# The first FFN's residual sum in a fused transformer-like kernel: one VectorE operation becomes a ScalarE and a GpSimd one

## The reference

```python
x = x + 0.5 * ffn(layernorm(x))
x = x + attn(layernorm(x))          # gated convolution, linear recurrence, product, residual, layernorm * ln_w + ln_b
x = x + 0.5 * ffn(layernorm(x))     # the same weights
# ffn: router logits -> sigmoid + bias -> best 2 of 4 groups -> best 4 of 32 experts, weights scaled by 2.5
#      sum over all chosen experts of w * down(silu(gate x) * (up x)), inner size 64, plus one shared expert of inner size 128
```

## Time and profile before

| | us |
|---|---|
| median of 3 runs | 675.33 (675.2 to 675.62) |
| the profiled execution | 675.38 |
| its span, first to last instruction | 673.6 |
| TensorE busy in it | 659.0 (98%) |
| VectorE busy | 550.5 (82%) |
| ScalarE busy | 421.5 (63%) |
| GpSimd busy | 446.5 (66%) |

### The profile page before, as it was taken

The page is one execution under the profiler, slowest core; times in us unless marked ns, Lnnn a source line. Parts: engine busy times, 40 slices in busy tenths (PEclk is TensorE's granted clock), DMA queues, the critical chain, the costliest instruction groups (busy, mean ns, idle before and its releaser), DMA issues. The chain is left out here.

```text
span 673.6 us, 10309 instructions
## 1 busy us (share of the span) xinstructions
PE 659.0 (98%) x3071; PEld 532.7 (79%) x3071; DVE 550.5 (82%) x1540; ACT 421.5 (63%) x804; POOL 446.5 (66%) x452
## 2 busy tenths in 40 slices
PE   7999999999999999999999999999999999999997
PEld 6877888888888887888878888888878778777685
DVE  5788889988978887889779898688979868867765
ACT  3766576675576656666567765757576566655553
POOL 2256558775676776866767766878676776776563
PEclk7999999999999999999999999999999999999999
DMA  7752908429092834719074370916519064380561
GB/s 191 168 139 68 224 4 195 91 71 199 5 210 72 185 85 96 159 58 224 20 176 111 89 166 26 228 35 154 116 30 221 5 157 108 76 184 17 119 135 32
DMA packets 60232, 78.30 MB, mean 116 GB/s; under 512 B 8176, under 2 KB 27664, under 8 KB 60176
## 3 DMA queue, kind: packets, MB, share of 16 engines
q1 hardware_dynamic: 60176, 77.65, 51.6%
HBM read 74.49 MB, written 3.15 MB: 115 GB/s over the span
## 5 line engine op out<-in xcount | busy, mean ns | idle before, releaser
L578 POOL TENSOR_TENSOR hid_lo<-hid,hid_hi 128x512 fp32r<-128x512 f32 x270 | 348.3, 1294 | 191.5 <-ACT hid_hi L690 191.3
L837 DVE TENSOR_TENSOR weighted<-gate_ps,raw 128x512 f32<-128x512 f32 x256 | 175.3, 685 | 69.3 <-ACT gate_ps L682 62.0
L682 ACT ACTIVATE gate_ps<-gate_ps 128x512 f32<-128x512 f32 x256 | 148.7, 581 | 120.0 <-PE gate_ps L1116 116.6
L690 ACT ACTIVATE hid_hi<-hid 128x512 fp32r<-128x512 f32 x272 | 170.5, 627 | 62.6 <-DVE hid L850 59.3
L850 DVE TENSOR_TENSOR hid<-weighted,up_ps 128x512 f32<-128x512 f32 x256 | 174.3, 681 | 7.5
L1177 PE MATMUL down_ps<-hid_lo,wt_hi 128*128 128x512 f32 x272 | 107.8, 396 | 0.2 <-DVE hid_lo L858 0.2
L1174 PE MATMUL down_ps<-hid_hi,wt_hi 128*128 128x512 f32 x272 | 107.7, 396 | 0.0
L1175 PE MATMUL down_ps<-hid_hi,wt_lo 128*128 128x512 f32 x272 | 107.5, 395 | 0.0
L1114 PE MATMUL gate_ps<-xT_hi,wt_hi 128*128 128x512 f32 x170 | 71.7, 422 | 0.0
L1114 PE MATMUL up_ps<-xT_hi,wt_hi 128*128 128x512 f32 x170 | 68.2, 401 | 2.1 <-DVE hid L850 2.1
L1115 PE MATMUL gate_ps<-xT_lo,wt_hi 128*128 128x512 f32 x170 | 67.2, 395 | 0.0
(11 more groups left out here) (183 smaller groups left out, 1114.6 us busy)
## 6 DMA issues: line engine op xcount, KB each, us to landing
raw<-wT_hbm SPq DMA_DIRECT2D x96, 512.0 KB, 11.4
raw<-wT_hbm SPq DMA_DIRECT2D x62, 256.0 KB, 4.6
x_ln<-in_L_attn_x SPq DMA_DIRECT2D x8, 256.0 KB, 4.0
x_res<-in_L_attn_x SPq DMA_DIRECT2D x8, 256.0 KB, 3.7
out_x<-x SPq DMA_DIRECT2D x7, 256.0 KB, 2.3
raw<-in_L_ffn_gate_w SPq DMA_DIRECT2D x4, 256.0 KB, 5.2
raw<-in_L_ffn_up_w SPq DMA_DIRECT2D x4, 256.0 KB, 4.4
raw<-in_L_ffn_down_w SPq DMA_DIRECT2D x4, 256.0 KB, 4.7
```

What stands on the lines that cost most here:

```text
L578: nc.gpsimd.tensor_tensor(hid_lo[s][:, :], hid[s][:, :], hid_hi[s][:, :].bitcast(F32), ALU.subtract)\
L682: nc.scalar.activation(bank[:, :] if j else silu_sb[:, :], bank[:, :], ACT.Silu).then_inc(silu_done, 1)
L690: nc.scalar.activation(hid_hi[s][:, :], hid[s][:, :], ACT.Copy).then_inc(hid_hi_done, 1)
L837: V.tensor_tensor(weighted[j % 2][:, :], gate_ps[n % BANKS][:, :], wb[:, j - 1, :], ALU.mult)\
```

## The change

ScalarE reads `side` with a factor 0.5 into a new SBUF tile `first_half`; GpSimd adds `x_res` to it. VectorE's operation goes. TensorE's next use of `side` waits for ScalarE's read in place of VectorE's sum. In the tables, "add ffn 1" goes to the next whole slot, and in units (1,1) and (1,2) the steps from "stats 2" to "normalise 2" (in (1,2) to "transpose 2") go to later slots.

```diff
-        ADD = {"copy ffn 1": 1, "transpose ffn 1": 4, "add ffn 1": 8.5}
+        ADD = {"copy ffn 1": 1, "transpose ffn 1": 4, "add ffn 1": 9, "halve ffn 1": 5}
...
# BEGIN, unit (1,1), block 0
-                ({"copy ffn 1": 2, "transpose ffn 1": 3, "add ffn 1": 5.5}, 0),
-                ({"stats 2": 5.5, "meanvar 2": 5.5, "norm 2": 6, "normalise 2": 7, "transpose 2": 10, "xT high 2": 10,
+                ({"copy ffn 1": 2, "transpose ffn 1": 3, "add ffn 1": 6, "halve ffn 1": 4}, 0),
+                ({"stats 2": 7.5, "meanvar 2": 7.5, "norm 2": 8, "normalise 2": 9, "transpose 2": 10, "xT high 2": 10,
...
# BEGIN, unit (1,2), block 1
-                ({"copy ffn 1": 3, "transpose ffn 1": 4, "add ffn 1": 4.5}, 1),
-                ({"stats 2": 5.5, "meanvar 2": 5.5, "norm 2": 6, "normalise 2": 7, "transpose 2": 8, "xT high 2": 10,
+                ({"copy ffn 1": 3, "transpose ffn 1": 4, "add ffn 1": 5, "halve ffn 1": 5}, 1),
+                ({"stats 2": 6.5, "meanvar 2": 6.5, "norm 2": 7, "normalise 2": 8, "transpose 2": 9, "xT high 2": 10,
...
# BEGIN, unit (1,3), block 2
-                ({"copy ffn 1": 1, "transpose ffn 1": 4, "add ffn 1": 3.5}, 2),
+                ({"copy ffn 1": 1, "transpose ffn 1": 4, "add ffn 1": 5, "halve ffn 1": 5}, 2),
...
# END, unit (4,4), block 7
-                ({"copy ffn 1": 3, "transpose ffn 1": 4, "add ffn 1": 6.5}, 7),
+                ({"copy ffn 1": 3, "transpose ffn 1": 4, "add ffn 1": 7, "halve ffn 1": 5}, 7),
...
# GpSimd, behind "norm 2" and ahead of "add ln_b"
+                    for b in due(steps, "add ffn 1", j):
+                        pool.wait_ge(x_res_loaded, b * 16 + 16)
+                        pool.wait_ge(first_halved, b + 1)
+                        if b >= 2:
+                            pool.wait_ge(x1_b_done, b - 1)
+                            pool.wait_ge(ln_normed[2], b - 1)
+                        nc.gpsimd.tensor_tensor(x1[b % 2][:, :, :], first_half[:, :, :], x_res[:, :, :], ALU.add)\
+                          .then_inc(ffn_added[1], 1)
...
# ScalarE, behind "xT high 1" and ahead of "copy ffn 1"
+            def halve_first(b):
+                act.wait_ge(ffn_transposed[1], b + 1)
+                if b > 0:
+                    act.wait_ge(ffn_added[1], b)
+                nc.scalar.activation(first_half[:, :, :], side_td, ACT.Copy, scale=0.5).then_inc(first_halved, 1)
...
# VectorE
-                for b in due(steps, "add ffn 1", slot):
-                    dve.wait_ge(x_res_loaded, b * 16 + 16)
-                    dve.wait_ge(ffn_transposed[1], b + 1)
-                    if b >= 2:
-                        dve.wait_ge(x1_b_done, b - 1)
-                    V.scalar_tensor_tensor(x1[b % 2][:, :, :], side_td, 0.5, x_res[:, :, :], ALU.mult, ALU.add)\
-                     .then_inc(ffn_added[1], 1)
...
# TensorE
-                        side_read = (ffn_added[1], b + 1)
+                        side_read = (first_halved, b + 1)
```

More of the change, by code:

```diff
@@ L208, in macaron_kernel @@
         ffn_half = sb("ffn_half", [P, TT, P])
+        first_half = sb("first_half", [P, TT, P])
         gate_t = sb("gate_t", [P, BLK])
@@ L297, in macaron_kernel @@
         halved_done = sem("halved_done")
+        first_halved = sem("first_halved")
         y_hi_done = sem("y_hi_done")
@@ L751, in unit @@
                         xT_high(1, b)
+                    for b in due(steps, "halve ffn 1", j):
+                        halve_first(b)
                     for b in due(steps, "copy ffn 1", j):
```

## The result

The changed kernel took 678.84 us (median of 5 runs, 677.4 to 679.54) against 675.33 us before: ratio 1.0052, 95% interval 1.0041 to 1.0063, so 3.5 us slower. It lies in the range given, one microsecond above the number predicted; two of the five executions, the profiled one among them, lie above the range's end of 679.2.

The account below looks back on a forecast made before the run. TensorE, almost never idle, was taken to bound the kernel, so only its waits count. The terms 2.4 + 0.4 - 0.3 gave +2.5 us on the profiled 675.38, so 677.9, with a range of 675.0 to 679.2.

Parts of the forecast that it names:

- What bounds the kernel: Whole kernel: TensorE is busy 659.0 of 673.6 us, so time freed on VectorE is worth nothing by itself.
- The shared-table units, 0: The four units of blocks 3 to 6: idle time covers the added operations; 0, bounds 0 to 0.2 us each.
- The second rival: Shared-table units: GpSimd's additions hold VectorE's operation with two SBUF inputs, 4 x 0.6 us, total 680.3; chance 0.04.
- the rule of the Trainium skill: VectorE operations with both inputs in SBUF and GpSimd instructions reading SBUF share a read interface; the later one is blocked.
- Unit (1,2), the main term: Unit (1,2): TensorE waits for "normalise 2" before "transpose 2"; +2.4 us, bounds 1.6 to 3.3.
- GpSimd is in time: Unit (1,2): GpSimd has "norm 2" done at 129.75, before "normalise 2" starts on ScalarE at 129.87.
- Behind the wait everything on the other engines catches up, so I count it once: Unit (1,2): the 2.4 us wait is counted once, as the other engines catch up behind it.
- the upper bound of 3.3: Unit (1,2): the term's upper limit, should late silu and weighting cause a second wait at tile 11.
- Unit (1,1): Unit (1,1): "transpose 2", due at 89.81, waits for "normalise 2" until 90.2; +0.4 us, bounds 0 and 1.0.
- Unit (4,4): Unit (4,4): the bank is read earlier, so "mixer out" no longer waits; -0.3 us, bounds -0.5 and +0.3.
- No wait at all (1): Units (1,2) and (1,1): no wait, time stays or falls by the 0.3 of (4,4), 675.1; chance 0.13.
- VectorE the real pace (3): Whole kernel: VectorE sets the pace, TensorE's records hide it, and 5.5 us come back, 669.9; chance 0.04.

Follow-up runs that it names:

- The doubling: The changed kernel with ScalarE's halving and GpSimd's addition done twice for blocks 3 to 6; 678.57 us.
- the filled wait: The changed kernel with ten extra TensorE products right ahead of the waited-for "transpose 2" of unit (1,2); 677.97 us, ratio 1.0038.
- the early sum alone: The kernel before with only VectorE's sum of block 7 in unit (4,4) moved from slot 6.5 to 5.5; 674.8 us, ratio 0.9997.
- the early halving: The changed kernel with halving and addition right behind the transpose in (1,1) and (1,2), later steps in their old slots; 674.94 us, ratio 0.9990.

## Why the prediction was right
**What bounds the kernel.** Right: nothing that VectorE gave up came back as such, and the result is where TensorE waits. The ledger has it to a tenth.

**The shared-table units, 0.** Right. In unit (4,2), ScalarE's and GpSimd's timelines of the changed kernel, which answer to the earlier trace rows:

```profile
364.18 0.58 ACT L717 ACTIVATE first_half<-side 128x512 f32<-128x512 f32 x1
364.66 0.59 ACT L692 ACTIVATE gate_ps<-gate_ps 128x512 f32<-128x512 f32 x1
365.55 0.63 ACT L700 ACTIVATE hid_hi<-hid 128x512 fp32r<-128x512 f32 x1 [0.30 <-DVE hid L868]
```
```profile
372.75 1.31 POOL L632 TENSOR_TENSOR x<-first_half,x_res 128x512 f32<-128x512 f32 x1
374.05 1.29 POOL L580 TENSOR_TENSOR hid_lo<-hid,hid_hi 128x512 fp32r<-128x512 f32 x1
```

ScalarE's idle time ahead of `hid_hi` shrank from 0.79 to 0.30, and VectorE is no later. The `hid_lo` at 374.05 is where the earlier trace rows has it, 4.26 later like the unit: the addition fits its gap of 1.25 us. The doubling says that at least as much room again was left. The second rival (GpSimd's additions hold VectorE's operation with two SBUF inputs) had no effect: the two don't meet. In (4,2) VectorE's operation starts at 368.60, the addition at 372.75. So the rule of the Trainium skill, page "SBUF — State Buffer", section "Who interferes with whom", is not contradicted.

**Unit (1,2), the main term.** The mechanism and the wait were right: 2.4 predicted, 2.39 measured. The chain came as worked out. ScalarE's timeline, the answer to the earlier trace rows:

```profile
128.27 0.63 ACT L700 ACTIVATE hid_hi<-hid 128x512 fp32r<-128x512 f32 x1 [1.34 <-DVE hid L868]
128.81 1.64 ACT L741 ACTIVATE normed<-res,shift,rstd 128x128 f32<-128x128 f32 x4
130.39 1.65 ACT L741 ACTIVATE normed<-x,shift,rstd 128x128 f32<-128x128 f32 x4
131.95 0.57 ACT L692 ACTIVATE gate_ps<-gate_ps 128x512 f32<-128x512 f32 x1
```

Predicted, with the unit 0.5 earlier: 127.8, 128.3, 129.87. "GpSimd is in time" was right by a hair: 0.12 us to spare in the working, 0.03 in the trace (130.36 against 130.39). What the term left out is the clock: "Behind the wait everything on the other engines catches up, so I count it once" is true of the other engines and not of TensorE itself, which went on at half its clock for 3.4 us. This is the step that was wrong, a cost put at nothing: the unit's +4.13 lies above the upper bound of 3.3, and that bound had been set for another reason. With its 1.64 us the term would have been 4.0. The Trainium skill, page "TensorE: Matmul & The Clock Gate", section "Part 1: The HAM clock gate (the "warmup" mystery)", has the two levels and says that idleness brings the lower one; the filled wait agrees with it. The kernel before, whose longest wait of TensorE behind the setup was 1.0 us, shows no fall there.

**Unit (1,1).** 0.4 predicted, a wait of 0.44, the unit 0.63 longer; within its bounds.

**Unit (4,4) and the rest.** -0.3 predicted, -0.38 measured, by the release of the bank (shown by the early sum alone). The -0.13 in (1,3) and -0.25 in (1,5) were not predicted. They are in every kernel with the new form and in none with VectorE's sum. In (1,5) it is TensorE's wait for `w_tok` at the trace's 337 us that goes; why this unit alone had it is open.

**The rivals.** No wait at all (1): false for this change, although the early halving shows that the form as such could have had it. GpSimd's additions holding VectorE in the shared-table units (2): false, those units kept their length. VectorE the real pace (3): false.

**Sum.** +2.5 predicted, +3.5 by the medians, +4.0 between the profiled executions. The terms' signs and places were right; the clock is the 1.64 that is missing. That the median still lies in the range is in part luck: no term and no bound held a fall of the clock, the profiled execution, 679.39, lies above the range's end, and in one of the two fastest executions the clock most likely did not fall.

## What to carry to other kernels
Where one engine has almost no idle time, as here, taking work from another gains nothing by itself, and what counts is when the busy engine's inputs come. So follow the steps that were moved, not the operations that were exchanged: in an issue order written by hand, a step put one slot later also goes behind all that already stands in that slot, here a second "stats" and a second normalisation. When a sum becomes two operations on other engines, look for their idle time directly behind the producer before anything downstream is moved; that was the difference between +3.5 and -0.4 us.

## What the runs showed of the hardware
A single gap of 2.4 us between TensorE's products, with 100 us of work ahead of it that only shorter waits broke, was followed in all four traces that have it by 3.4 us at a granted clock of 0.50. That cost another 1.64 us, two thirds as much again as the gap; by the mean clocks on record it most likely did not happen in every execution. The other gaps behind the setup, the longest 1.93 us between products (in (4,7) of the early halving, a wait of 1.76), left the clock at 1.00 in these traces; no gap of a length between these two occurs in them. Ten products whose result is thrown away, in the place of the wait, kept the clock at 1.00 in their trace; the median was 0.9 us lower (677.97 against 678.84), with overlapping ranges.
